# An edge stage on one NeuronCore: operands of the VectorE products in PSUM, and one PSUM bank for sums and join

## The reference

```python
def mlp(x, Wh, bh, Wo, bo, ln_w, ln_b):
    for i in range(3):
        x = relu(x @ Wh[i] + bh[i])
    return layernorm(x @ Wo + bo) * ln_w + ln_b
fs, fr = mlp_flux(x[src]), mlp_flux(x[dst])          # 64 channels x 2
a = mlp_a((x[src] + x[dst]) * 0.5)                   # 64 channels
flux = 0.5 * (fs . nvec + fr . nvec) - 0.5 * a * (x[src] - x[dst])
out = layernorm(x + segment_sum(flux, dst))
```

## Time and profile before

| | |
|---|---|
| median of 3 runs | 7842.77 us (7839.77 to 7843.71) |
| the profiled execution's own time | 7838.6 us |
| its span | 7836.2 us |
| granted TensorE clock, mean | 0.857 |
| busy share: TensorE, VectorE, ScalarE, GpSimd | 72%, 59%, 33%, 75% |
| gathers of the edge stage | 3153.6 to 7761.5 us of the span |

### The profile page before, as it was taken

The page is one execution under the profiler, slowest core; times in us unless marked ns, Lnnn a source line. Parts: engine busy times, 40 slices in busy tenths (PEclk is TensorE's granted clock), DMA queues, the critical chain, the costliest instruction groups (busy, mean ns, idle before and its releaser), DMA issues. The chain is left out here.

```text
span 7836.2 us, 158560 instructions
## 1 busy us (share of the span) xinstructions
PE 5666.6 (72%) x50020; PEld 4530.6 (58%) x50222; DVE 4624.3 (59%) x8442; ACT 2573.8 (33%) x5044; POOL 5851.4 (75%) x5108
## 2 busy tenths in 40 slices
PE   2799999899999999466666666656666666666665
PEld 2699999899999989333333333333333333333333
DVE  7899999422224444555556555556555555555555
ACT  0689888400001111232222222232222222222222
POOL 5788888577766665777777777777777777777774
PEclk6899999999999999787777777787778777777777
DMA  5343343565656665555555555555555555555553
GB/s 138 134 146 139 134 145 129 193 230 210 224 209 215 204 207 192 140 145 145 145 145 146 145 145 145 147 148 147 145 145 145 146 149 145 145 144 145 145 144 99
DMA packets 599972, 1231.69 MB, mean 157 GB/s; under 512 B 329609, under 2 KB 408757, under 8 KB 582195
## 3 DMA queue, kind: packets, MB, share of 16 engines
q0 software_dynamic: 214272, 618.71, 30.4%
q1 hardware_dynamic: 369606, 576.65, 21.5%
q10 hardware_dynamic: 15485, 29.03, 1.3%
HBM read 1026.18 MB, written 197.69 MB: 156 GB/s over the span
## 5 line engine op out<-in xcount | busy, mean ns | idle before, releaser
L1773 POOL DMA_INDIRECT edge_rows<-node_table,edge_et x3224 | 3626.1, 1125 | 985.0 <-issue 948.9
L1790 PE MATMUL edge_tp<-ident,edge_yc 128*128 128x128 f32 x1612 | 585.2, 376 | 1787.6 <-ACT edge_h L1868 1747.8
L816 POOL DMA_INDIRECT two_rows<-x_parts,src_at x1120 | 1090.2, 973 | 574.3 <-issue 358.5
L1291 PE MATMUL two_acc<-x_parts,two_win 128*128 128x192 bf16 x16072 | 1398.4, 248 | 44.5 <-issue 27.3
L1790 PEld LDWEIGHTS edge_tp<-ident,edge_yc 128*128 128x128 f32 x1612 | 303.5, 188 | 1878.4 <-issue 1641.4
L1291 PEld LDWEIGHTS two_acc<-x_parts,two_win 128*128 128x128 fp8e4 x16072 | 1353.6, 99 | 58.3 <-issue 46.5
L1862 ACT ACTIVATE edge_yc<-edge_rows 128x512 f32<-128x512 f32 x403 | 253.6, 630 | 3278.1 <-DMA edge_rows<-node_table,edge_et 3240.3
L1801 PE MATMUL edge_mp<-edge_h,edge_W 128*128 128x512 f32 x1612 | 1309.1, 960 | 2.3 <-ACT edge_h L1868 2.3
L1983 DVE TENSOR_REDUCE edge_ssq<-edge_sq 128x8 f32<-128x512 f32 x403 | 276.4, 686 | 1618.6 <-ACT edge_sq L1875 1618.6
L1049 ACT ACTIVATE one_win<-one_count 128x784 fp8e4<-128x784 f32 x1312 | 1070.6, 825 | 130.3 <-PE one_count L1000 65.1
L816 POOL DMA_INDIRECT one_rows<-x_parts,src_at x560 | 875.1, 1563 | 170.7 <-issue 170.7
(11 more groups left out here) (319 smaller groups left out, 6993.3 us busy)
## 6 DMA issues: line engine op xcount, KB each, us to landing
two_win<-adjacency SPq DMA_DIRECT2D x82, 3136.0 KB
adjacency<-one_win SPq DMA_DIRECT2D x41, 3136.0 KB
edge_near<-near_ids SPq DMA_DIRECT2D x403, 192.0 KB
edge_rows<-node_table,edge_et POOLq DMA_INDIRECT x3224
two_rows<-x_parts,src_at POOLq DMA_INDIRECT x1120
node_table<-two_row SPq DMA_DIRECT2D x49, 322.0 KB
edge_own<-node_table SPq DMA_DIRECT2D x46, 322.0 KB
node_sums<-edge_seg SPq DMA_DIRECT2D x806, 16.2 KB
```

Source lines behind the costliest of these rows:

```text
L816: pool.indirect_dma_start(rows[:, b % 2, e, :], None, XP.rearrange("p (j c) -> (p j) c", c=3 * C), bass.IndirectOffsetOnAxis(ap=src_at[:, ...
L1291: mm = pe.matmul(acc[b][:, half * 3 * C:(half + 1) * 3 * C], win[:, b, half, j, :].bitcast(FP8), now[:, j, :], start=(j == 0), stop=(j == ...
L1773: pool.indirect_dma_start(rows[:, h.b, t, :], None, T5, bass.IndirectOffsetOnAxis(ap=et[:, h.b, 0, t:t + 1].bitcast(I32), axis=0))\
L1790: pe.matmul(to, yc[:, h.b % 2, 2 * pr:2 * pr + 2, :].rearrange("p t c -> p (t c)"), ident[:, :], is_transpose=True, start=True, stop=False)
```

## The change

VectorE's and TensorE's use of the eight PSUM banks is rearranged. The sums and the join share one bank (sums_ps), so that sums of a chunk now also waits until take_raw has emptied the sums of the chunk before, and take_raw waits for the join of the chunk before. The two banks that this frees hold part (128 x 8 x 64 floats) and kept, in which the constant ramp and two buffers of the edge vectors nvec lie.

In VectorE's stages: a small copy puts nvec of the chunk into kept; the mask sel reads the ramp from PSUM. flux is four operations of 512 elements (F1 x nvec into part, F0 x nvec, part - B into part, F0 + part). The product of zp with x moves into squared and writes part; scale multiplies part by the reciprocal root, forms the scaled zp in X_Y as before, and subtracts part from the flux. In each of these operations one input lies in PSUM and one in SBUF. ScalarE gets a copy of nvec into the columns X_N, and its take_raw comes behind the first two relus. SyncE waits for that copy, eight chunks back, before it loads the edge table.

```diff
-        raw_ps = [ps(f"raw{b}", [P, 512])[:, 0:SC] for b in range(2)]
-        fold_ps = ps("fold_ps", [P, 512])[0:2 * NW, 0:SC]
+        sums_ps, part, kept = ps("sums_ps", [P, 512]), ps("part", [P, TL, C]), ps("kept", [P, 512])
+        raw_ps, fold_ps = sums_ps[:, 0:SC], sums_ps[0:2 * NW, 256:256 + SC]
+        ramp_ps = kept[:, 0:NW]
+        n_ps = [kept[:, NW + 2 * TL * b:NW + 2 * TL * (b + 1)].rearrange("p (d t) -> p d t", d=2) for b in range(2)]
-                 "zp_made zp_used sq_made ssq_made std_made order_v v_made weighed scaled raw_made raw_out edge_set fold_made seg_out stored padded storing base_in "
+                 "zp_made zp_used sq_made ssq_made std_made order_v v_made n_kept n_made weighed scaled raw_made raw_out edge_set fold_made seg_out stored padded storing base_in "
...
+                    sp.sem_inc(sems["storing"], 1)
+                    sp.wait_ge(sems["n_made"], h.c - RB + 1)
...
             def sums(h):
+                pe.wait_ge(sems["n_made"], h.c + 1)
+                if not early(h, 1):
+                    pe.wait_ge(sems["raw_out"], h.c)
-                    pe.wait_ge(sems["raw_out"], h.c - 1)
+                    pe.wait_ge(sems["seg_out"], h.c - 1)
                 for turn_of in range(2):
-                        mm = pe.matmul(raw_ps[h.b % 2][q * NW:(q + 1) * NW, :], sel[:, h.b, t, :], rows[:, h.b, t, 0:SC],
+                        mm = pe.matmul(raw_ps[q * NW:(q + 1) * NW, :], sel[:, h.b, t, :], rows[:, h.b, t, 0:SC],
...
+                act.activation(rows[:, h.b, :, X_N:X_N + 2], et[:, h.b, 2:4, :].rearrange("p d t -> p t d"), ACT.Copy)\
+                    .then_inc(sems["n_made"], 1)
             def relu(h, i):
...
             def take_raw(h):
-                if not early(h, 3):
-                    act.wait_ge(sems["fold_made"], h.c - 2)
-                act.activation(raw_rows[:, h.b % 4, :], raw_ps[h.b % 2], ACT.Copy).then_inc(sems["raw_out"], 1)
+                if not early(h, 1):
+                    act.wait_ge(sems["fold_made"], h.c)
+                act.activation(raw_rows[:, h.b % 4, :], raw_ps, ACT.Copy).then_inc(sems["raw_out"], 1)
             def take(h):
...
-            stages = ((4, squares), (6, take_raw), (1, lambda h: relu(h, 0)), (2, lambda h: relu(h, 1)), (4, root), (3, lambda h: relu(h, 2)), (7, take))
+            stages = ((4, squares), (1, lambda h: relu(h, 0)), (2, lambda h: relu(h, 1)), (6, take_raw), (4, root), (3, lambda h: relu(h, 2)), (7, take))
             chunks(act, step, HS, RB, DONE_LAG)
...
+            o.link(dve.tensor_copy(ramp_ps, ramp[:, :]))
...
-                dve.tensor_tensor(sel[:, h.b, :, :], ramp[:, :].unsqueeze(1).broadcast_to([P, TL, NW]),
+                dve.tensor_copy(n_ps[h.b % 2], et[:, h.b, 2:4, :]).then_inc(sems["n_kept"], 1)
+                dve.tensor_tensor(sel[:, h.b, :, :], ramp_ps.unsqueeze(1).broadcast_to([P, TL, NW]),
             def flux(h):
-                both = rows[:, h.b, :, X_F0:X_F1 + C].rearrange("p t (d c) -> p t d c", d=2)
-                dve.tensor_tensor(both, both, et[:, h.b, 2:4, :].rearrange("p d t -> p t d").unsqueeze(3).broadcast_to([P, TL, 2, C + 1]), ALU.mult)\
-                    .then_inc(sems["order_v"], 1)
-                dve.wait_ge(sems["order_v"], 2 * h.c + 1)
+                dve.wait_ge(sems["n_kept"], h.c + 1)
+                n0, n1 = (n_ps[h.b % 2][:, i, :].unsqueeze(2).broadcast_to([P, TL, C]) for i in range(2))
-                dve.tensor_tensor(to, to, rows[:, h.b, :, X_F1:X_F1 + C], ALU.add).then_inc(sems["order_v"], 1)
-                dve.wait_ge(sems["order_v"], 2 * h.c + 2)
-                dve.tensor_tensor(to, to, rows[:, h.b, :, X_B:X_B + C], ALU.subtract).then_inc(sems["v_made"], 1)
+                if not early(h, 1):
+                    dve.wait_ge(sems["v_made"], h.c)
+                if not early(h, LAG):
+                    dve.wait_ge(sems["scaled"], h.c - LAG + 1)
+                dve.tensor_tensor(part[:, :, :], rows[:, h.b, :, X_F1:X_F1 + C], n1, ALU.mult).then_inc(sems["order_v"], 1)
+                dve.tensor_tensor(to, to, n0, ALU.mult).then_inc(sems["order_v"], 1)
+                dve.wait_ge(sems["order_v"], 3 * h.c + 1)
+                dve.tensor_tensor(part[:, :, :], part[:, :, :], rows[:, h.b, :, X_B:X_B + C], ALU.subtract).then_inc(sems["order_v"], 1)
+                dve.wait_ge(sems["order_v"], 3 * h.c + 3)
+                dve.tensor_tensor(to, to, part[:, :, :], ALU.add).then_inc(sems["v_made"], 1)
             def squared(h):
...
+                dve.wait_ge(sems["v_made"], min(h.c + LAG, HS) if isinstance(h.c, int) else h.c + LAG)
+                if not early(h, 1):
+                    dve.wait_ge(sems["scaled"], h.c)
+                dve.tensor_tensor(part[:, :, :], zp[b][:, :, :], rows[:, h.b, :, X_W:X_W + C], ALU.mult).then_inc(sems["weighed"], 1)
...
-                w = rows[:, h.b, :, X_Y:X_Y + C]
-                dve.tensor_tensor(w, zp[b][:, :, :], ssq[:, b, :].unsqueeze(2).broadcast_to([P, TL, C]), ALU.mult).then_inc(sems["zp_used"], 1)
-                dve.wait_ge(sems["zp_used"], h.c + 1)
-                own_x = rows[:, h.b, :, X_W:X_W + C]
-                dve.tensor_tensor(own_x, own_x, w, ALU.mult).then_inc(sems["weighed"], 1)
-                dve.wait_ge(sems["weighed"], h.c + 1)
+                root = ssq[:, b, :].unsqueeze(2).broadcast_to([P, TL, C])
+                dve.wait_ge(sems["weighed"], 2 * h.c + 1)
+                dve.tensor_tensor(part[:, :, :], part[:, :, :], root, ALU.mult).then_inc(sems["weighed"], 1)
+                dve.tensor_tensor(rows[:, h.b, :, X_Y:X_Y + C], zp[b][:, :, :], root, ALU.mult).then_inc(sems["zp_used"], 1)
+                dve.wait_ge(sems["weighed"], 2 * h.c + 2)
-                dve.tensor_tensor(to, to, own_x, ALU.subtract).then_inc(sems["scaled"], 1)
+                dve.tensor_tensor(to, to, part[:, :, :], ALU.subtract).then_inc(sems["scaled"], 1)
```

## The result

The changed kernel takes 7273.86 us (median of four runs, 7266.41 to 7278.63) against 7842.08 for the kernel before: ratio 0.9275, 95% interval 0.9259 to 0.9291. The forecast was 7299 with a range of 7262 to 7400.

What follows compares the result with a forecast made beforehand. GpSimd's eight gathers per step were taken as the bound. Profiled 7838.6 us - 576.2 (gathers) + 30 (remaining holds) + 3 (end) = 7295.4; with 4.2 for the runs' median, forecast 7299 us, range 7262 to 7400.

Steps and rivals of the forecast that it cites:

- What bounds the kernel: Edge stage: GpSimd's eight gathers per step, with 0.30 us gaps, alone set its length, 11.4 us.
- The cause: Gathers averaging 1125 ns instead of 946 are held by VectorE instructions with two SBUF inputs until those end.
- The moment at +0.13 us: A gather needs something 0.13 us after starting; a two-SBUF-input VectorE instruction running then holds it.
- The gathers, -576.2 us: With the holding VectorE instructions gone, 3224 gathers fall to 0.946 us each: 3049.9 us against 3626.1.
- What still holds, +30 us: Edge stage: remaining holds on gathers, 19 us from finishing-work products at random phase and 12 us from tensor_scalar L1960.
- The covers: Added work and waits on VectorE, ScalarE, TensorE and SyncE fit within the 10.0 us step: 0 us each.
- The end, +3 us: After the last gather, steps run at TensorE's and VectorE's pace; more VectorE work in four of them adds 3 us.
- (1): Edge stage: L1960 takes over as holder of gathers in most steps, +129 us, 7428 us; chance 0.08.
- (2): VectorE operations with SBUF operand first and PSUM second still hold gathers, gain only 214 us, 7629 us; chance 0.03.
- (3): VectorE or TensorE becomes the bound near 10 us; mean step 10.4 us, +150 us, 7450 us; chance 0.06.
- (4): Nothing happens: gathers are held by something other than two SBUF inputs, 7843 us; chance 0.01.
- (5): PSUM traffic at half rate lengthens VectorE's products until VectorE sets the pace: +140 us, 7983 us; chance 0.02.

Runs made afterwards that it cites:

- the pair of probes: Changed kernel plus one unused 1024-element VectorE product per step, second input in PSUM or in SBUF: 7275.34 us and 7610.87 us.
- the probe: Changed kernel plus one unused 1024-element VectorE product per step before the first flux product, both inputs in SBUF: 7610.87 us, ratio 0.9688.
- sel_t_psum: Changed kernel with mask sel_t made by a tensor_tensor against the node column in PSUM instead of a tensor_scalar: 7265.24 us, ratio 0.9251.
- bank_only: Kernel before with only the shared PSUM bank, its waits and take_raw's new place, on another chip: 9593.66 us against 9584.73, ratio 1.0007.
- probe_psum_again: Changed kernel plus one unused 1024-element VectorE product per step, one input in SBUF and one in PSUM: 7275.34 us, ratio 0.9264.

## Why the prediction was right

**What bounds the kernel.** Right: the gathers' gap stayed 0.30 us and all of the gain is in their length.

**The cause.** Right. The direct test is the pair of probes: the same instruction, 0 us or +335.5 us by the place of one operand. The moment at +0.13 us was wrong as a rule for what begins beside a gather. L2000 begins within the first 0.13 us of a gather 18 times in the kernel before and holds none, and the probe holds all 100 at which it begins 0.25 to 0.35 us late. That a held gather ends 0.82 us after the holder does is right, and the sum needed no more than that.

**The gathers, -576.2 us.** The floor of 946 ns is the median and was reached. Of the holders that I named L1975 holds none in the trace of before: L1971, just ahead of it, has held the gather by then. As all of them went, this changed nothing.

**What still holds, +30 us.** It is 3066.9 - 3224 x 0.946 = 17.0 us. I had taken 12 us for the mask and 19 for the finishing work. The 15.0 us that sel_t_psum takes away are nearly all of it, and in the changed kernel's trace 14.6 us go to the mask, by 72 gathers that end 0.82 us after it and 52 that end some 0.12 us after it: the mask accounts for most, and the finishing work was mis-sized. With the mask out of the way all the finishing work costs 1.4 us, where random phase had given 19. The mask is also held itself by gathers, 518 ns in the mean at a median of 477, which I had not thought of; its share of the gathers' time is small, and VectorE has 2.5 us of waiting per step to take it up.

**The covers.** VectorE's chain in the plain step that begins at 5024.56 ends with L1993 at 5031.61, 7.05 us; I had 7.4 to 8.1. No price for PSUM, right to 10 ns. TensorE and ScalarE: the shared bank costs nothing, by bank_only at 12.2 us a step and by the gathers' gap at 10.05. SyncE: covered on the chip of the result, and the part where I was blind: on other chips the rows point to it as the engine that takes over.

**The end, +3 us.** It is +0.1 us.

**The sum.** The profiled execution was to take 7295.4 us and took 7269.2: 13 us from the holds, 10 from the earlier stages' spread, 3 from the end.

**The rivals.** (1) L1960 as the holder: it holds, but a small part. It begins 0.40 to 0.90 us after a gather's start, the place worked out for it, in 232 of the 403 steps. (2) The order of operands: none, by L1988 and L1989 in the timeline and by the mean of 951 ns. (3) Another engine: not on this kind of chip; probe_psum_again adds 1.2 us per step free. (4) and (5): out, by the result and by the 676 to 700 ns. That the pace could go to SyncE's queue was in none of them; I had costed it with the durations of one chip.

## What to carry to other kernels

When GpSimd's indirect DMAs set the pace, look at the spread of their durations, not at the mean: a median at the floor beside a mean of 1125 ns says that something holds some of them, and the VectorE instruction that ends 0.82 us before each long one says what. A VectorE operation with two SBUF inputs is then not free even if VectorE is idle half of the time; one operand in PSUM made it free here, at the same duration. Before counting on it, look at what is next in line: with the gathers at their floor, the other engines' queues decide, and on two of the chips seen here the time went up by 4 to 6%, with SyncE's queue the likely limit.

## What was not expected of the hardware

- A gather can be held by an instruction that starts after it: 2.30 us for one that had started 0.27 us before a 1.21 us product. Not every such instruction does this: L2000, at the same distance, left all 79 gathers at 0.95 us.
- A one-input copy of four-byte elements in SBUF holds a gather in its last part also (it ends 0.12 or 0.13 us after the copy), the two-input product only in its first part (0.82 us before its end).
- It goes both ways: the mask of 477 ns took up to 723 ns beside a gather.
- The same kernel before took 7842, 9585 and 9783 us on different chips, and the changed operands gave -7% on the first kind and +4 to +6% on the others.
